# Rotary projection of a grouped attention layer: halves of two heads in one tile instead of two halves of one head

## What is computed

```
h = rmsnorm(x, ln_w)
q = (h @ wq).reshape(B, S, 16, 128)
k = (h @ wk).reshape(B, S, 4, 128)
v = (h @ wv).reshape(B, S, 4, 128)
ang = pos[:, None] * inv_freq[None, :]          # 512 x 64
q = apply_rope(q, cos(ang), sin(ang))           # pairs (x1, x2) = even and odd features of a head
k = apply_rope(k, cos(ang), sin(ang))           # r1 = x1 cos - x2 sin ; r2 = x1 sin + x2 cos
scores = einsum('bqhd,bkhd->bhqk', q, k) / sqrt(128)
```

## Time and profile before

| | us |
|---|---|
| median of 3 runs | 2533.64 |
| lowest, highest | 2531.52, 2536.02 |
| profiled execution, its own time | 2537.47 |
| its span (first to last instruction) | 2535.6 |
| TensorE, VectorE, ScalarE, GpSimd busy in the span | 2010.2, 1670.2, 1222.4, 729.7 |
| mean granted clock of TensorE, share of full speed | 0.854 |
| stage of the change, first load issued to the attention's first load issued | 1251.8 to 1486.5 |

### The profile page before, as it was taken

One profiled execution on the slowest core, in us unless ns is written; L12 is line 12 of the kernel. 1 busy time (PEld: TensorE's weight loads), 2 busy tenths in 40 slices (PEclk: granted clock), 3 DMA queues, 4 the chain that ended last, 5 costly groups with the idle time before them and its releaser, 6 DMA issues. The chain is left out here.

```text
span 2535.6 us, 41622 instructions
## 1 busy us (share of the span) xinstructions
PE 2010.2 (79%) x12514; PEld 1565.1 (62%) x12514; DVE 1670.2 (66%) x3522; ACT 1222.4 (48%) x2616; POOL 729.7 (29%) x817
## 2 busy tenths in 40 slices
PE   6599986399999765887477769999979807999990
PEld 3366645299999632332355537677759707999990
DVE  5344426788888775785678767777754416888865
ACT  1144431244444312777145448888863206777750
POOL 3022222255555430000145544444430140000005
PEclk9555556699999976999789889999989758999995
DMA  3511100000000025220122223222236316555523
GB/s 122 115 52 52 51 8 1 33 17 25 25 25 17 0 92 120 59 62 25 71 83 83 99 112 109 83 108 107 83 132 213 112 66 243 207 207 213 215 106 99
DMA packets 93281, 231.54 MB, mean 91 GB/s; under 512 B 13456, under 2 KB 39184, under 8 KB 86032
## 3 DMA queue, kind: packets, MB, share of 16 engines
q1 hardware_dynamic: 88976, 220.59, 25.2%
q0 software_dynamic: 3072, 8.39, 1.0%
q10 hardware_dynamic: 1152, 1.57, 0.5%
HBM read 157.10 MB, written 72.88 MB: 91 GB/s over the span
## 5 line engine op out<-in xcount | busy, mean ns | idle before, releaser
L544 POOL TENSOR_SCALAR d_att_probs<-d_att_probs,d_att_rinv 128x128 f32<-128x128 f32 (+2 forms) x192 | 177.6, 925 | 219.2 <-DVE d_att_rinv L555 219.1
L1439 DVE SCALAR_TENSOR_TENSOR b_acc<-bank,b_gates,b_acc 128x256 f32<-128x256 f32 x512 | 212.4, 477 | 41.7 <-PE bank L1354 41.7
L1407 POOL TENSOR_TENSOR b_moe_act_low<-b_moe_act,b_moe_act_high 128x512 fp32r<-128x512 f32 x136 | 175.9, 1294 | 177.5 <-ACT b_moe_act_high L1384 177.5
L434 PE MATMUL wide<-d_att_k,d_att_q 128*128 128x128 f32 (+3 forms) x512 | 188.1, 450 | 18.7 <-DMA d_att_k<-k_dram 18.5
L2017 PE MATMUL wide<-e_moe_hT_high,e_moe_w_high 128*128 128x256 f32 x644 | 183.2, 284 | 14.2 <-DVE e_moe_w_low L2087 14.2
L913 DVE TENSOR_REDUCE a_att_rmax<-wide 128x2 f32<-128x256 f32 (+3 forms) x128 | 104.7, 824 | 130.2 <-PE wide L706 129.6
L913 DVE TENSOR_REDUCE c_att_rmax<-wide 128x2 f32<-128x1024 f32 x128 | 155.3, 1223 | 49.9 <-PE wide L698 45.2
L2017 PE MATMUL wide<-e_moe_hT_high,e_moe_w_low 128*128 128x256 f32 x644 | 183.0, 284 | 0.0
L2017 PE MATMUL wide<-e_moe_hT_low,e_moe_w_high 128*128 128x256 f32 x644 | 183.0, 284 | 0.0
L491 ACT ACTIVATE d_att_probs<-wide,d_att_nmax 128x128 f32<-128x128 f32 (+3 forms) x256 | 135.4, 529 | 78.8 <-DVE d_att_nmax L550 78.8
L829 ACT ACTIVATE c_att_probs<-bank 128x512 f32<-128x512 f32 x256 | 139.1, 596 | 56.8 <-PE bank L736 52.3
(11 more groups left out here) (361 smaller groups left out, 6172.8 us busy)
## 6 DMA issues: line engine op xcount, KB each, us to landing
e_moe_w<-in_e_w SPq DMA_DIRECT2D x23, 2688.0 KB, 9.8
q_dram<-d_in_rot SPq DMA_DIRECT2D x16, 1024.0 KB, 3.9
d_att_q<-q_dram SPq DMA_DIRECT2D x16, 1024.0 KB, 4.9
o_dram<-d_att_o SPq DMA_DIRECT2D x64, 256.0 KB, 2.0
d_out_oT<-o_dram SPq DMA_DIRECT2D x16, 1024.0 KB, 5.6
b_moe_w<-in_b_w SPq DMA_DIRECT2D x17, 512.0 KB, 3.4
a_q<-q_parts SPq DMA_DIRECT2D x96, 64.0 KB, 2.2
c_q<-q_parts SPq DMA_DIRECT2D x96, 64.0 KB, 2.2
```

The lines of the kernel that those rows point to most:

```text
L434: nc.tensor.matmul(stile[qt], qs[s][:, u, qt * P:(qt + 1) * P], ks[s][:, 0, 0:w], start=True, stop=False)
L544: g.tensor_scalar(tile, tile, rinv[:, j, qt:qt + 1], None, ALU.mult).then_inc(scaled, 1)
L1407: g.tensor_tensor(ap[1][:, u % 4, :], act[:, u % 4, :], ap[0][:, u % 4, :], ALU.subtract).then_inc(act_low, 1)
L1439: nc.vector.scalar_tensor_tensor(out=tile, in0=y, scalar=gate, in1=tile, op0=ALU.mult, op1=ALU.add).then_inc(acc_done, 1)
```

## The change

The weights' columns are laid out so that a tile holds one half of each of two heads. Tile 2p holds the even features (x1) of heads 2p and 2p + 1, one head in partitions 0 to 63 and the other in 64 to 127. Tile 2p + 1 holds their odd features (x2), in the same partitions. No swap of partitions is left: ScalarE's copies and `xw` go.

VectorE does one instruction for each tile. It reads the PSUM tile twice (a dimension of step 0) and multiplies it by two neighbouring rows of a rope table of three rows (-sin, cos, sin): tile 2p gives x1 cos and x1 sin (`first`), tile 2p + 1 gives -x2 sin and x2 cos (`second`). GpSimd adds the two for the pair of tiles in one instruction of 128 x 1024: the first 512 are r1 of both heads, the others r2. The buffers `first` and `second` exist twice, for p % 2. The rope table is loaded with 3072 numbers for each partition instead of 2048.

In DRAM a head has the layout that it had. So a quad of heads is stored by four transfers of 64 partitions x 2 x 512. The z and h of the next batch stand behind pair 2 (tile 5) and pair 6 (tile 13), the roots behind adds of pairs 0 and 3. `terms` counts one for each tile.

```diff
-                    for cc in range(NC):
-                        v.wait_ge(swapped, b * NC + (cc + 1))
-                        v.wait_ge(rot_ready, b * NC + (cc + 1))
-                        nc.vector.tensor_tensor(xc[:, cc % 2, :], ps[cc % 4][:, :], rope[:, cc // H, 0, :], ALU.mult).then_inc(terms, 1)
-                        nc.vector.tensor_tensor(xs[:, cc % 2, :], xw[:, cc % 4, :], rope[:, cc // H, 1, :], ALU.mult).then_inc(terms, 1)
-                        if cc == 5 and not last:
+                    for p in range(PAIRS):
+                        kind = 2 * p // H
+                        v.wait_ge(rot_ready, b * PAIRS + (p + 1))
+                        for i, (out, lo) in enumerate(((first, 1), (second, 0))):
+                            cc = 2 * p + i
+                            v.wait_ge(qk_done, b * NC + (cc + 1))
+                            nc.vector.tensor_tensor(out[:, p % 2, :, :], ps[cc % 4][:, :].unsqueeze(1).to_broadcast([P, 2, S]),
+                                                    rope[:, kind, lo:lo + 2, :], ALU.mult).then_inc(terms, 1)
+                        if p == 2 and not last:
                             keep_z(b + 1)
-                        if cc == 12 and not last:
+                        if p == 6 and not last:
                             keep_h(b + 1)
...
-                    for cc in range(NC):
-                        g.wait_ge(terms, 2 * NC * b + (2 * cc + 10))
-                        if cc % 4 == 0:
-                            g.wait_ge(stored[cc // 4], 16 * b + 16)
-                        g.tensor_tensor(rot[:, cc, :], xc[:, cc % 2, :], xs[:, cc % 2, :], ALU.add).then_inc(rot_ready, 1)
-                        if cc == 1 and not last:
+                    for p in range(PAIRS):
+                        g.wait_ge(terms, NC * b + (2 * p + 2 + 4))
+                        if p % 2 == 0:
+                            g.wait_ge(stored[p // 2], 64 * b + 64)
+                        g.tensor_tensor(rot[:, 2 * p:2 * p + 2, :], first[:, p % 2, :, :], second[:, p % 2, :, :], ALU.add).then_inc(rot_ready, 1)
+                        if p == 0 and not last:
                             norm_x.root(g, b + 1)
-                        if cc == 6 and not last:
+                        if p == 3 and not last:
                             norm_z.root(g, b + 1, rms=True)
...
-                    for cc in range(NC):
-                        s.wait_ge(qk_done, b * NC + (cc + 1))
-                        nc.scalar.copy(xw[0:HALF, cc % 4, :], ps[cc % 4][HALF:P, :])
-                        nc.scalar.copy(xw[HALF:P, cc % 4, :], ps[cc % 4][0:HALF, :]).then_inc(swapped, 1)
...
-                        pe.wait_ge(terms, 2 * NC * b + (2 * cc + 2))
+                        pe.wait_ge(terms, NC * b + (cc + 1))
...
-                        sp.wait_ge(rot_ready, b * NC + (4 * quad + 4 + 2))
-                        if quad < 4:
-                            dst = q_dram[bass.ds(4 * b + quad, 1), :, :, :].rearrange("a p u s -> p (a u) s")
-                        else:
-                            dst = k_dram[bass.ds(4 * b, 4), :, :, :].rearrange("g p u s -> p (g u) s")
-                        sp.dma_start(dst, rot[:, 4 * quad:4 * quad + 4, :]).then_inc(stored[quad], 16)
+                        sp.wait_ge(rot_ready, b * PAIRS + (2 * quad + 2 + 2))
+                        for pair in range(2):
+                            for half in range(2):
+                                if quad < 4:
+                                    dst = q_dram[bass.ds(4 * b + quad, 1), :, 2 * pair + half, :]
+                                else:
+                                    dst = k_dram[bass.ds(4 * b + (2 * pair + half), 1), :, 0, :]
+                                cc = 4 * quad + 2 * pair
+                                sp.dma_start(dst.rearrange("a (r p) s -> p (a r) s", r=2), rot[HALF * half:HALF * (half + 1), cc:cc + 2, :]
+                                             ).then_inc(stored[quad], 16)
```

More of the change, by code:

```diff
@@ L1502, in grouped_projection @@
     NC = H + KVH
+    PAIRS = NC // 2
     HALF = P // 2
@@ L1514, in grouped_projection @@
         wv = [sb(f"wv_{part}", [P, KT, KVH * GD], F32R) for part in ("high", "low")]
-        col, rope = sb("col", [P, KT]), sb("rope", [P, 2, 2, S])
+        col, rope = sb("col", [P, KT]), sb("rope", [P, 2, 3, S])
         h = sb("h", [P, NQ, D])
         hT = [sb(f"hT_{part}", [P, KT, S], F32R) for part in ("high", "low")]
-        xw = sb("xw", [P, 4, S])
-        xc, xs = sb("xc", [P, 2, S]), sb("xs", [P, 2, S])
+        first, second = sb("first", [P, 2, 2, S]), sb("second", [P, 2, 2, S])
         rot = sb("rot", [P, NC, S])
@@ L1537, in _ @@
                 for quad in range(5):
-                    sp.sem_inc(stored[quad], 16)
+                    sp.sem_inc(stored[quad], 64)
                 for dst, src in ((raw_v, weights(a["d_wv"])), (col[:, :], a["d_ln"])):
@@ L1690, in _ @@
                 pe.sem_inc(tr_done, KT)
-                pe.sem_inc(terms, 8)
+                pe.sem_inc(terms, 4)
                 turn(0)
@@ L2276, in laid_out, with rotated_pairs @@
     b_w = np.concatenate([w1, w2.transpose(0, 2, 1)], axis=2)
-    evens_first = np.concatenate([np.arange(0, GD, 2), np.arange(1, GD, 2)])
-    wq = i["L1_ffn_wq"].reshape(D, H, GD)[:, :, evens_first].reshape(D, H * GD)
-    wk = i["L1_ffn_wk"].reshape(D, KVH, GD)[:, :, evens_first].reshape(D, KVH * GD)
+    def rotated_pairs(w):
+        heads = w.shape[1] // GD
+        return w.reshape(D, heads // 2, 2, GD // 2, 2).transpose(0, 1, 4, 2, 3).reshape(D, heads * GD)
+    wq, wk = rotated_pairs(i["L1_ffn_wq"]), rotated_pairs(i["L1_ffn_wk"])
     inv_freq = np.float32(1e6) ** (-np.arange(0, GD, 2, dtype=np.float32) / np.float32(GD))
     angle = (np.arange(S, dtype=np.float32)[:, None] * inv_freq[None, :]).T.astype(np.float64)
-    rope = np.stack([np.concatenate([np.cos(angle), np.cos(angle)]),
-                     np.concatenate([-np.sin(angle), np.sin(angle)])], axis=1)
+    angle = np.concatenate([angle, angle])
+    rope = np.stack([-np.sin(angle), np.cos(angle), np.sin(angle)], axis=1)
     rope = np.stack([rope / np.sqrt(GD), rope], axis=1).astype(np.float32)
```

6 lines of the change are left out of this document (3 added, 3 removed).

## The result

The changed kernel takes 2496.52 us in the median of four runs (2495.3 to 2499.53), against 2534.39 (2531.52 to 2536.02) for the kernel before beside it. The ratio is 0.985, with a 95% interval of 0.983 to 0.986: 37.9 us less. The interval is clear of 1, though the gain is under 2%. The forecast was 2498, with a range of 2482 to 2514. The profiled execution took 2495.3, with a span of 2493.4; TensorE's granted clock is 0.854 in the mean, as before.

The account below looks back on a forecast made before the run. The bound was taken to be VectorE's `xs` and GpSimd's add excluding each other. Savings of 26.4 (three iterations) and 9.9 (the last), less 1 for stores, gave 35.3 us less: 2498 us, range 2482 to 2514.

Parts of the forecast that it names:

- The exclusion of `xs` and the add: VectorE's `xs`, with two SBUF inputs, and GpSimd's add go one after the other: 1.92 us a tile.
- Prices: Costs in the stage: new product 1.22 us, unheld by adds; new add 2.41; root 1.35; ScalarE's two copies of 0.58 go.
- z and h: VectorE's SBUF-only instructions for the next batch wait out GpSimd's longer add, each 1.12 us longer: 4.0 and 3.3.
- The iteration: From TensorE's tile 0, the next v matmuls begin at 39.3 us instead of 48.08: 8.8 less, three times, 26.4.
- The v matmuls: TensorE's matmuls ahead of tile 0, 7.11 us in the iteration read; no saving was counted for them.
- The last iteration: Without z and h, TensorE paces it: the last add ends at 31.9 us instead of 41.84, 9.9 less.
- Stores: Only the stage's last four stores count, issued at 0.38 us each, the fourth 1.14 later: +1 us, at most some +11.
- A: On VectorE, z and h slip between GpSimd's adds, costing about 1.4 and 1.2 us: 50 less, 2483; chance 0.15.
- B: Handover in pairs is dearer, product 1.36 and add 2.58 us: 27 less, 2506; chance 0.16 with its store tail.
- C: VectorE's product reading PSUM twice is held off by GpSimd's add, 4.67 us a pair: 27 more, 2561; chance 0.04.

## Why the prediction was right, step by step

In sum the stage lost 37.9, where 35.3 was worked out. The terms were off by +2.9 (iterations), +0.1 (last iteration), -0.7 (stores) and +0.2 (v matmuls), so the gain was some 2.6 larger than worked out. The forecast of the median is off by only 1.5 since the kernel before, measured again beside the changed one, came out 0.8 above the median from which the forecast was taken.

- **The exclusion of `xs` and the add is the bound.** Right, and shown from both sides: lifting it alone gives 32.9 of 37.7, putting it back costs 55. The Trainium skill's rule (SBUF — State Buffer, Who interferes with whom) holds in both directions: the product is held in the form with two SBUF inputs (3.41) and not in the form with one in PSUM (1.224 median, 1.206 least).
- **Prices.** Product 1.22: measured 1.224. Add 2.41: 2.410. Reading PSUM twice by a step of 0 costs nothing. Copies worth 1.2 an iteration: 6.8 for four, so 1.7 each.
- **z and h.** 4.0 and 3.3: measured 3.63 and 3.27. z was issued 9.75 after tile 0 (9.7 worked out). The sizes are a little high. The working had z pass through adds 1 and 2 and end at 13.8, and it did, at 13.4. But the price beside it, "each waits 1.12 longer" for one longer add, was drawn too simply: not one add but the whole backlog holds z. (The add beside z before, read as 1.29, took 1.39; that changes nothing here.)
- **The iteration.** Tile 12 at 24.15 (25.0), last product done at 36.8 (37.9), v matmuls at 38.3 (39.3), so 29.3 saved over three iterations and not 26.4. Most of that 1.0 an iteration is in one price, used twice: the roots take 1.02 instead of 1.35. The root of x stands ahead of the adds that z waits for, so z ends 0.4 sooner, and the root of z stands ahead of add 4, for which tile 12 waits. The 1.35 was a mean over one root of 1.01 and three of 1.47 that `xs` had lengthened: a price that holds a wait was carried into a kernel without that wait, and the free one stood in the same trace.
- **The v matmuls** were carried over unchanged. They differ by up to 1.3 in single iterations, but by 0.2 in the sum. The forecast was lucky there: over the runs of the table the sum goes from 25.5 to 33.4.
- **The last iteration.** 31.9 worked out, 31.85 measured, adds 2.8 apart.
- **Stores.** +1 worked out, +1.7 measured. The term was made with 0.38 for an issue. The half-partition stores take 0.60 each to issue and start 0.79 apart (3.02 for four), so the last is 2.4 later, not 1.14. The last four land 3.2, 3.3, 3.8 and 3.6 after their start, where 1 MB took 4.3 and a 128-partition store of the same bytes 2.0. That agrees in its direction with the pages (the Trainium skill, SBUF — State Buffer, Door 1: The DMA port swizzle), where the estimated 1.3 was of moving alone. A store that starts with no other in flight takes 3.2 too (the one at 1397.59), so 1.2 over the row of 2.0 belongs to the form itself. How much of that is the half of the ports and how much the shape, no run here separates. The later ones of a quad, with others in flight, take up to 0.9 more.
- **Rivals.** A (z slips between the adds) did not come: v to v is 45.5 to 46.8, not 41. B's prices didn't either. C was refuted for this form and reproduced in the form with SBUF operands.

Among the forecasts of the experiments, those of h (8.0 of 9 in the rest) and of the early z (30.8 for 31, in two of three iterations) were good, that of the copies by some luck. Right in kind and off in size were the operand (35.6 and not 40 to 44), the single instruction (2.3 and not 3 to 4) and the bias on GpSimd (32.7 and not 31.5). Three missed: z by a shorter add (the backlog), the SBUF form (55 and not 69), and z on ScalarE (34.6 and not 31, in part by a small instruction held like a large one). All three missed on how VectorE and GpSimd take turns.

## What to carry to other kernels

If an instruction of VectorE has a minimum of half its median beside a working GpSimd, look where its operands are: here one of them read from PSUM instead of SBUF was worth 33 us, and half as many products 2.3. An instruction's duration from a trace may hold a wait; use the minimum (the root: 1.01, against a mean of 1.35), or one from a stretch in which the other engine rests, if the change removes that wait. When an engine comes free, move to it what the bound engine does in SBUF beside GpSimd's work, and see that no small instruction is left there as a link in the chain.
